# Masks of attention scores in row halves, value products ahead of transposes, and one root-mean-square pair per item

## The chip, the cores and the metric

The kernel runs on one core of one Trainium2 chip. The metric is the device time of one execution in microseconds (us), here the median of several runs. One more execution was recorded by the hardware profiler, and every row below is from it. The engines are TensorE (PE; its weight loads are listed apart as PEld), VectorE (DVE), ScalarE (ACT), GpSimd (POOL) and SyncE (SP).

## The reference

64 items of audio go through a convolution tower (four convolutions with channel norms), an importance pooling that leaves 128 rows of 64 numbers per item, causal attention, and a mixture of experts. Only the attention is touched by the change:

```python
x = layernorm(h)                                   # (64, 128, 64)
q = (x @ wq.T) as 16 heads of 64; k, v = x @ wkv.T # one key/value head for all 16
q = rmsnorm(rope(q), q_norm_w); k = rmsnorm(rope(k), k_norm_w)
scores = q @ k.T / 8                               # 128 x 128 per head
scores = where((cols <= rows) & (rows - cols <= 128), scores, -1e30)   # causal: T is 128
h = h + (softmax(scores) @ v over the heads) @ wo.T
```

So each of 64 items has 16 heads with a 128 x 128 score matrix, 1024 such matrices in all.

## The kernel before

The program has a convolution phase (0 to about 720 us) and a token phase, which interleaves three streams by an order written out by hand: importance and pooling, attention, experts. Each engine walks the same list of slots `u` and issues in each slot what is planned for it. Work goes from engine to engine by semaphores, and each engine does its instructions strictly in order.

In the attention a slot is one *part* (four heads of one item): 256 slots, from 1034 us to about 1740 us. Two slots make a *half* `m` (eight heads); scores are issued once a half, on even slots. Below, "pair" means these two slots, and pairs are numbered by `m % 8`, since everything repeats after 8 pairs (4 items, a *quad*). In steady state an item passes through these steps:

- **Queries.** `project(m)` (L1163, L1164) makes eight heads of queries in PSUM; DVE applies the rotation (`rope_q`, L1277 to L1279); ACT squares (`square`, L1417) and DVE sums the squares (`sum_q`, L1310); ACT makes the reciprocal root by a Ln and an Exp (`rms_q`, L1423 and L1428), once a half; POOL adds the two rotated products (`add_q`, L1545) and multiplies by the root (`scale_q`, L1552); PE transposes (`q_t`, L1173) and ACT copies out (`keep_q`, L1435). The slots are in the tables `at_q`, `at_rms`, `at_qm`, `at_qt`.
- **Scores.** `scores(m)` fills two PSUM banks. For each bank, one bf16 matmul of the identity with the mask (128 rows, 512 columns; L1186) writes the mask, and then the products with the keys are added (L1191). These use 64 rows of the array, the two banks' products in different row halves. Three banks rotate, so `scores(m)` waits for the exponentials of part `2m-2`.
- **Softmax.** DVE takes the negated maximum (`maximum`, L1317), ACT the exponentials with their sums (`exps`, L1446), DVE the reciprocal (`recip`, L1325), POOL multiplies (`normalize`, L1559).
- **Transposes and value products.** PE transposes each part three slots later (`p_t`, L1203) into the one bank TB, DVE copies it out (`p_copy`, L1332), and the next `p_t` waits for that copy. `p_v` (L1214) multiplies eight heads by the values, on even slots: two column halves of the array of 64 columns each. `w_o` (L1224) is the output projection of a quad, of the same column halves, in four pieces `c`, in slots 6, 7, 8 and 9 of every 16.
- **Once a quad** PE also does `x_t`, `k_v`, `k_t` and `turn` (L1131 to L1151, L1234), DVE `rope_k`, `sum_k`, `residual`, `statistics`, and POOL the preparation of the keys and of the next quad's input.

The order in a slot on PE is: `scores`, `p_t`, `project`, `q_t`, `x_t`, `k_v`, `k_t`, `w_o`, `turn`, `p_v`. On DVE: `maximum(u)`, `recip(u-1)`, `p_copy(u-3)`, `rope_q`, `sum_q`, then the quad's pieces. On ACT: `keep_o`, `square`, `keep_q`, `rms_q`, the quad's pieces, `exps(u)`. On POOL: `normalize(u-1)`, `add_q`, `scale_q`, the quad's pieces.

Of the kernel before, what the change touches and what calls it, by code (L numbers as in the profile page):

```python
# [8 lines left out]
BF16 = mybir.dt.bfloat16  # L9
F32R = mybir.dt.float32r  # L10
U32 = mybir.dt.uint32
ALU = mybir.AluOpType
# [4 lines left out]
B = 64  # L17
# [6 lines left out]
NH, DH = 16, 64  # L24
# [18 lines left out]
          ("riota", 8), ("eps0", 1), ("scaled", 1)]  # L43
# [26 lines left out]
def audio_tower(nc, A, out):  # L70
    const_at, n_const = offsets(CONSTS)
    with ExitStack() as ctx:
# [3 lines left out]
        def sem(name):  # L76
# [35 lines left out]
        identb = sb("identb", [128, 128], BF16)  # L112
        maskb = sb("maskb", [128, 4, 128], BF16)
# [14 lines left out]
                 cs=cs, mv=mv, rstd=rstd, wqkv=wqkv, wo=wo, wqk=wqk, identb=identb, maskb=maskb, fcol=fcol, fwr=fwr,  # L128
# [489 lines left out]
def importance_pool_phase(nc, V, sem, ctx):  # L618
# [252 lines left out]
    def vector(ve):  # L871
# [81 lines left out]
        def stats4(i):  # L953
# [7 lines left out]
            for r in range(4):  # L961
# [3 lines left out]
        ve.tensor_copy(V["identb"][:], K["ident"])  # L965
        ve.tensor_copy(V["maskb"][:], K["mask"].unsqueeze(1).to_broadcast([128, 4, 128]))
        ve.scalar_tensor_tensor(out=V["wqk"][:], in0=V["qkw"][:, 0:DH], scalar=float(DH) ** -0.5,
                                in1=V["qkw"][:, DH:2 * DH], op0=ALU.mult, op1=ALU.mult)
# [69 lines left out]
def attention_phase(nc, V, sem, ctx, kept, pool):  # L1038
# [4 lines left out]
    wqkv, wo, wqk, identb, maskb = V["wqkv"], V["wo"], V["wqk"], V["identb"], V["maskb"]  # L1043
# [25 lines left out]
    at_q = by_slot(HALVES, lambda m: 4 * (m // 2) - 11 + 2 * (m % 2))  # L1069
    at_rms = by_slot(HALVES, lambda m: 4 * (m // 2) - 9 + 2 * (m % 2))  # L1070
# [4 lines left out]
    at_wo = {16 * (q + 1) + 6 + c: (q, c) for q in range(QUADS) for c in range(4)}  # L1075
# [43 lines left out]
    def tensor(pe):  # L1119
# [57 lines left out]
        def scores(m):  # L1177
# [7 lines left out]
            for bank in banks:  # L1185
                pe.matmul(bank, identb[:], maskb[:].rearrange("p a s -> p (a s)"), start=True, stop=False,  # L1186
                          skip_group_check=True)
# [9 lines left out]
        def p_t(n):  # L1197
            i, k = n // 4, n % 4
            if n >= 1:
                pe.wait_ge(S["pT"], n)  # L1200
            pe.wait_ge(S["pn"], n + 1)
            for h in range(4):
                last = pe.transpose(ps[:, TB, h * T:(h + 1) * T], pb[:, i % 2, 4 * k + h, :], K["ident"])  # L1203
            last.then_inc(S["pt"], 1)

# [32 lines left out]
        def slot(u):  # L1238
# [9 lines left out]
            if u == min(at_pt):  # L1248
                pe.wait_ge(made["h4"], QUADS)
            if u == min(at_pv):  # L1250
                pe.wait_ge(made["wx"], QUADS)
            if u in at_pt:
                p_t(at_pt[u])
# [19 lines left out]
    def vector(ve):  # L1273
# [83 lines left out]
        def prepare():  # L1357
            high, low = split(ve, wh[:], wl[:], wqkv[:])
# [30 lines left out]
    def scalar(ac):  # L1389
# [74 lines left out]
        def slot(u):  # L1464
# [16 lines left out]
            if u - 1 in at_wo and at_wo[u - 1][1] == 3:  # L1481
                keep_y(at_wo[u - 1][0])
# [5 lines left out]
    def gpsimd(po):  # L1488
# [58 lines left out]
        def scale_q(m):  # L1547
            h = m % 2
            po.wait_ge(S["rq"], m + 1)
# [607 lines left out]
def shape_constants():  # L2157
# [8 lines left out]
            "ones": np.ones((128, 128)), "mask": np.where(j <= i, 0.0, -1e30),  # L2166
# [4 lines left out]
    return np.concatenate([np.asarray(cols[n], np.float32) for n, _ in CONSTS], 1)  # L2171
# [71 lines left out]
```

## Time and profile before

| | us |
|---|---|
| runs, median of 3 (1931.29 to 1932.2) | 1932.19 |
| profiled execution, its own time | 1930.25 |
| span of the profile (first to last instruction) | 1928.3 |
| PE busy / share | 1816.9 / 94% |
| DVE busy / share | 1525.3 / 79% |
| ACT busy / share | 1354.8 / 70% |
| POOL busy / share | 921.0 / 48% |

Busy times are unions of intervals over the whole span; the shares are averages over stages that differ. The mean granted clock of TensorE was 0.982 of its full speed.

### The profile page before, as it was taken

The page shows a single profiled execution, that of the slowest core. Times are in us where ns is not written, and L with a number is a line of the kernel's source. Part 1 is how long each engine was busy: PE and PEld are TensorE (multiplying, and loading weights), DVE is VectorE, ACT ScalarE, POOL GpSimd, SP SyncE. Part 2 cuts the span into 40 slices and gives each one's busy share as a digit, 9 for nine tenths or more (in the row PEclk, how much of TensorE's full clock was granted, in tenths as well). Part 3 has the DMA queues.
Part 4 walks back from the last instruction along what each step waited for, and adds up shares of the span by engine and source line. Part 5 has one row for each costly group of instructions (what it writes and reads, how often), then busy time and mean ns, then how long its engine had stood idle before and what let it go on. Part 6 is the DMA issues. An engine that isn't in the chain of part 4 may idle for free.

```text
span 1928.3 us, 35012 instructions
## 1 busy us (share of the span) xinstructions
PE 1816.9 (94%) x10533; PEld 1276.7 (66%) x10533; DVE 1525.3 (79%) x3372; ACT 1354.8 (70%) x3865; POOL 921.0 (48%) x1544
## 2 busy tenths in 40 slices
PE   3999999999999968999997999999999999999998
PEld 2777888888878856877875666666655555664443
DVE  5788888888888856566657888888999988896665
ACT  1567667767767653444436999999998999986765
POOL 1222322322322210022247989988888899983200
PEclk9999999999999988999987999999999999999999
DMA  3311111111111000000000000000000000004554
GB/s 97 96 45 38 34 47 37 35 49 34 37 47 34 25 1 1 0 1 1 1 1 1 2 2 2 2 2 2 1 2 2 2 2 2 2 2 181 188 214 166
DMA packets 30518, 69.02 MB, mean 36 GB/s; under 512 B 14108, under 2 KB 14748, under 8 KB 28028
## 3 DMA queue, kind: packets, MB, share of 16 engines
q1 hardware_dynamic: 30332, 66.78, 10.7%
q8 instruction: 87, 1.43, 0.3%
q14 instruction: 99, 0.81, 0.1%
HBM read 45.12 MB, written 2.36 MB: 25 GB/s over the span
## 4 chain that ended last, share of the span: by engine, by line
PE 37%; DVE 12%; issue 6%; POOL 4%; ACT 3%; DVEq 0%; POOLq 0%; ACTq 0%
PE ps L1191 4%; PE ps L65 4%; PE ps L1203 3%; PE ps L67 3%; PE ps L66 3%; PE ps L1224 3%; PE ps L1762 3%; PE ps L1214 2%; DVE amx L1317 2%; PE ps L1186 2%; DVE apT L1332 2%; PE ps L1173 2%; DVE assq L1310 1%; POOL apb L1559 1%; DVE atq L1277 1%
## 5 line engine op out<-in xcount | busy, mean ns | idle before, releaser
L1446 ACT ACTIVATE apb<-ps,amx 128x128 f32<-128x128 f32 x1024 | 360.0, 366 | 47.0 <-DVE amx L1317 46.5
L1559 POOL TENSOR_TENSOR apb<-apb,arc 128x512 f32<-128x512 f32 x256 | 268.4, 1048 | 43.9 <-DVE arc L1325 43.6
L1317 DVE TENSOR_REDUCE amx<-ps 128x4 f32<-128x512 f32 x256 | 174.4, 681 | 59.7 <-PE ps L1191 58.5
L1446 ACT ACTIVATION_READ_ACCUMULATOR apb<-ps,amx 128x1 f32 x1024 | 210.4, 205 | 0.0
L583 POOL TENSOR_TENSOR h0h<-h0h,const 128x1 fp32r<-128x1 f32 x256 | 46.6, 217 | 338.8 <-DVE h0l L479 338.8
L65 PE MATMUL ps<-h0h,w123h 128*128 128x512 f32 x512 | 203.0, 396 | 0.0
L67 PE MATMUL ps<-h0h,w123l 128*128 128x512 f32 x512 | 202.5, 396 | 0.0
L66 PE MATMUL ps<-h0l,w123h 128*128 128x512 f32 x512 | 202.5, 395 | 0.0
L1203 PEld LDWEIGHTS ps<-const,apb 128*128 128x128 f32 x1024 | 107.3, 140 | 135.9 <-DVE apT L1332 109.6
L479 DVE SCALAR_TENSOR_TENSOR h0l<-ps,h0h 128x1024 fp32r<-128x1024 f32 x128 | 156.0, 1219 | 46.3 <-ACT h0h L383 46.3
L1203 PE MATMUL ps<-const,apb 128*128 128x128 f32 x1024 | 167.6, 286 | 18.7 <-DVE apT L1332 18.0
L1332 DVE COPY apT<-ps 128x512 f32<-128x512 f32 x256 | 170.0, 664 | 6.8 <-PE ps L1203 6.5
L1191 PEld LDWEIGHTS ps<-akT,aqT 64*128 64x128 f32 x2048 | 125.0, 188 | 54.7 <-issue 54.7
L1191 PE MATMUL ps<-akT,aqT 64*128 64x128 f32 x2048 | 149.6, 286 | 0.0
L383 ACT ACTIVATE h0h<-ps 128x1024 fp32r<-128x1024 f32 x128 | 129.9, 1015 | 24.9 <-PE ps L307 24.9
L1214 PE MATMUL ps<-apT,avs 128*64 128x512 f32 x512 | 136.6, 612 | 0.0
L807 ACT ACTIVATE z<-ps,mcol 128x512 f32<-128x512 f32 x64 | 44.1, 689 | 114.8 <-PE ps L67 114.8
L1012 POOL TENSOR_TENSOR part<-cs,const 128x512 f32<-128x512 f32 x16 | 18.3, 1142 | 214.5 <-DVE cs L925 213.2
L67 PEld LDWEIGHTS ps<-h0h,w123l 128*128 128x128 f32 x512 | 97.0, 189 | 22.5
L66 PEld LDWEIGHTS ps<-h0l,w123h 128*128 128x128 f32 x512 | 97.4, 190 | 18.8
L1830 ACT ACTIVATE apb<-ps,mw 128x512 f32<-128x512 f32 x128 | 81.0, 687 | 40.8 <-PE ps L1749 40.5
L65 PEld LDWEIGHTS ps<-h0h,w123h 128*128 128x128 f32 x512 | 97.0, 189 | 18.8 <-DVE sq1b L498 0.4
(320 smaller groups left out, 5065.9 us busy)
## 6 DMA issues: line engine op xcount, KB each, us to landing
h<-gates SPq DMA_DIRECT2D x8, 2048.0 KB, 7.1
atq<-gates SPq DMA_DIRECT2D x8, 2048.0 KB, 7.3
x0k<-x0h SPq DMA_DIRECT2D x128, 72.0 KB
x<-in_x SPq DMA_DIRECT2D x32, 192.0 KB, 2.6
x0k<-x0l SPq DMA_DIRECT2D x64, 72.0 KB
x0k<-x0h SPq DMA_DIRECT2D x64, 48.0 KB
out<-akT SPq DMA_DIRECT2D x16, 128.0 KB, 1.9
x0k<-x0l SPq DMA_DIRECT2D x32, 48.0 KB
```

What stands on the lines that cost most here:

```text
L65: pe.matmul(out, wh, xh, start=start, stop=False)
L66: pe.matmul(out, wh, xl, start=False, stop=False)
L67: return pe.matmul(out, wl, xh, start=False, stop=stop)
L383: ac.activation(padded(h0h, row, half, i), ps[:, Y0:Y0 + 2, :], ACT.Relu).then_inc(s_h0h, 1)
L479: ve.scalar_tensor_tensor(out=padded(h0l, row, half, i), in0=ps[:, Y0:Y0 + 2, :], scalar=0.0, in1=padded(h0h, row, half, i).bitcast(F32), ...
L1191: last = pe.matmul(bank[:, p * T:(p + 1) * T], qT[rows, i % 2, 4 * h + p, :], kT[rows, i // 4 % 2, i % 4, :], start=False, stop=True, skip ...
L1203: last = pe.transpose(ps[:, TB, h * T:(h + 1) * T], pb[:, i % 2, 4 * k + h, :], K["ident"])
L1214: last = pe.matmul(ps[64 * odd:64 * odd + 64, OB, :], vs[:, i // 4 % 3, i % 4, :], pT[:, 8 * h + 4 * odd:8 * h + 4 * odd + 4, :], start=Tr ...
L1317: ve.tensor_reduce(mx[:, n % 4, :], ps[:, SB[n % 3], :].rearrange("p (h s) -> p h s", h=4), AX_X, ALU.max, negate=True).then_inc(S["mx"], 1)
L1332: ve.tensor_copy(pT[:, 4 * k:4 * k + 4, :], ps[:, TB, :].rearrange("p (h t) -> p h t", h=4)).then_inc(S["pT"], 1)
L1446: last = ac.activation(pb[:, i % 2, head, :], ps[:, SB[n % 3], h * T:(h + 1) * T], ACT.Exp, bias=mx[:, k, h:h + 1], accum_out=sm[:, i % 2, ...
L1559: po.tensor_tensor(p, p, rc[:, i % 2, 4 * k:4 * k + 4].unsqueeze(2).to_broadcast([T, 4, T]), ALU.mult).then_inc(S["pn"], 1)
```

## The change

- The mask of two banks is written by four matmuls in place of two. Each uses 64 rows and 256 columns (4 heads by 64 keys) of bf16; the bank of even heads uses the lower 64 rows, the other bank the upper ones, as the score products do. A new constant `maskt` (which row of the mask a query takes) and a folded `maskb` replace the identity and the full mask; they are made in `prepare`, in the middle of the importance phase, and `identb`, `maskb` and `wqk` are no longer made at the phase's start. Two constant columns are added.
- On PE the order in a slot becomes: `scores`, `p_v`, `w_o`, `p_t` on even slots, `project`, `q_t`, `x_t`, `k_v`, `k_t`, `turn`, `p_t` on odd slots. `w_o` has two pieces each in slots 6 and 8 in place of one in slots 6 to 9, and `keep_y` follows one slot earlier.
- `rms_q` does both halves of an item by one Ln and one Exp of 16 columns, in the slot of the first of the two before. `project`, `rope_q`, `square`, `sum_q` and `add_q` are two slots earlier.
- Waits that follow: `rms_q(i)`'s Exp waits for `scale_q` of both halves of the item before, and `sum_q` for the Ln of the item before.

```diff
-    at_q = by_slot(HALVES, lambda m: 4 * (m // 2) - 11 + 2 * (m % 2))
-    at_rms = by_slot(HALVES, lambda m: 4 * (m // 2) - 9 + 2 * (m % 2))
+    at_q = by_slot(HALVES, lambda m: 4 * (m // 2) - 13 + 2 * (m % 2))
+    at_rms = by_slot(B, lambda i: 4 * i - 9)
-    at_wo = {16 * (q + 1) + 6 + c: (q, c) for q in range(QUADS) for c in range(4)}
+    at_wo = {16 * (q + 1) + 6 + c: ((q, c), (q, c + 1)) for q in range(QUADS) for c in (0, 2)}
...
-            for bank in banks:
-                pe.matmul(bank, identb[:], maskb[:].rearrange("p a s -> p (a s)"), start=True, stop=False,
-                          skip_group_check=True)
+            for n in range(2):
+                for a, bank in enumerate(banks):
+                    rows = slice(a * DH, (a + 1) * DH)
+                    pe.matmul(bank.rearrange("p (h s) -> p h s", h=4)[:, :, n * DH:(n + 1) * DH], maskt[rows, n, :],
+                              maskb[rows, n, :, :], start=n == 0, stop=False, skip_group_check=True)
...
+            if u in at_pv:
+                p_v(at_pv[u])
+            for c in at_wo.get(u, ()):
+                w_o(*c)
+            if u % 2 == 0:
+                turn_p(u)
             if u in at_q:
                 project(at_q[u])
...
-            if u in at_wo:
-                w_o(*at_wo[u])
             if u in at_tr:
                 turn(at_tr[u])
-            if u in at_pv:
-                p_v(at_pv[u])
+            if u % 2 == 1:
+                turn_p(u)
...
-                ve.wait_ge(S["lrq"], m - 1)
+                ve.wait_ge(S["lrq"], i)
...
+            ve.tensor_copy(maskt[0:DH, 0, :], K["ident"][0:DH, :])
...
+            ve.tensor_copy(maskb[:], K["mask"].rearrange("p (n s) -> p n s", n=2).unsqueeze(2
+                                                                                         ).to_broadcast([T, 2, 4, DH]))
...
-        def rms_q(m):
-            i, h = m // 2, m % 2
-            heads = slice(8 * h, 8 * h + 8)
-            ac.wait_ge(S["ssq"], m + 1)
-            ac.activation(lrq[:, heads], ssq[:, heads], ACT.Ln, bias=epsc[:, 1:2], scale=1.0 / DH
-                          ).then_inc(S["lrq"], 1)
-            ac.wait_ge(S["lrq"], m + 1)
+        def rms_q(i):
+            ac.wait_ge(S["ssq"], 2 * i + 2)
+            ac.activation(lrq[:], ssq[:], ACT.Ln, bias=epsc[:, 1:2], scale=1.0 / DH).then_inc(S["lrq"], 1)
+            ac.wait_ge(S["lrq"], i + 1)
             if i >= 1:
-                ac.wait_ge(S["qm"], m - 1)
-            ac.activation(rq[:, heads], lrq[:, heads], ACT.Exp, scale=-0.5).then_inc(S["rq"], 1)
+                ac.wait_ge(S["qm"], 2 * i)
+            ac.activation(rq[:], lrq[:], ACT.Exp, scale=-0.5).then_inc(S["rq"], 1)
```

`turn_p(u)` is the old call of `p_t` with its wait, under a name.

## Rows read from the trace of the kernel before

**Rows 1.** Busy time of each engine in ten periods of attention: length, engines, clock, DMA.

```profile
1100.00:1540.00 440.00, 429.03 (x3226) 263.91 (x3224) 391.25 (x954) 400.30 (x1718) 393.08 (x399) 1.00 0.01 2
```

**Rows 2.** Waits in that stretch: who waited for whom, us, times, longest.

```profile
PEld ps L1203 <- DVE apT L1332: 69.4, 72, 1.9
```

**Rows 3.** PE's timeline over one period: start, us, instructions, [idle before].

```profile
1313.88 0.59 PE L1186 MATMUL ps<-maskb,identb 128*128 128x512 bf16 x2
...
1316.09 1.08 PE L1224 MATMUL ps<-h,wo 128*64 128x512 f32 x4
...
1319.44 1.08 PE L1224 MATMUL ps<-h,wo 128*64 128x512 f32 x4
...
1327.04 0.60 PE L1186 MATMUL ps<-maskb,identb 128*128 128x512 bf16 x2
1327.57 1.16 PE L1191 MATMUL ps<-akT,aqT 64*128 64x128 f32 x16
1328.66 0.66 PE L1203 MATMUL ps<-const,apb 128*128 128x128 f32 x4
1329.25 1.08 PE L1214 MATMUL ps<-apT,avs 128*64 128x512 f32 x4
1330.26 0.66 PE L1203 MATMUL ps<-const,apb 128*128 128x128 f32 x4
1330.67 0.47 PE L1163 MATMUL ps<-wh,axx 128*128 128x512 f32 x1
...
1331.65 0.60 PE L1234 MATMUL ps<-const,aysb 128*128 128x128 f32 x4
1332.09 0.59 PE L1186 MATMUL ps<-maskb,identb 128*128 128x512 bf16 x2
...
1337.16 0.59 PE L1186 MATMUL ps<-maskb,identb 128*128 128x512 bf16 x2
...
1342.01 0.59 PE L1186 MATMUL ps<-maskb,identb 128*128 128x512 bf16 x2
...
1347.91 0.61 PE L1186 MATMUL ps<-maskb,identb 128*128 128x512 bf16 x2
...
1352.54 0.59 PE L1186 MATMUL ps<-maskb,identb 128*128 128x512 bf16 x2
...
1356.47 0.66 PE L1203 MATMUL ps<-const,apb 128*128 128x128 f32 x4 [0.65 <-DVE apT L1332]
...
1357.87 0.59 PE L1186 MATMUL ps<-maskb,identb 128*128 128x512 bf16 x2
```

**Rows 4.** DVE's timeline over one pair: first and last instruction of ten.

```profile
1328.76 0.69 DVE L1317 TENSOR_REDUCE amx<-ps 128x4 f32<-128x512 f32 x1 [1.59 <-PE ps L1191]
...
1332.81 0.41 DVE L1279 TENSOR_TENSOR atq<-ps,const 128x256 f32<-128x256 f32 x1
```

**Rows 5.** ACT's timeline: the end of exponentials, and the Ln and Exp of the roots.

```profile
1319.49 0.21 ACT L1428 ACTIVATE arq<-alrq 128x8 f32<-128x8 f32 x1
...
1330.87 0.61 ACT L1455 ACTIVATE h<-ps 128x512 f32<-128x512 f32 x1
...
1331.35 0.32 ACT L1423 ACTIVATE alrq<-assq,epsc 128x8 f32<-128x8 f32 x1
1331.70 0.21 ACT L1428 ACTIVATE arq<-alrq 128x8 f32<-128x8 f32 x1
```

**Rows 6.** POOL's timeline: two multiplications of queries by their roots.

```profile
1318.96 1.05 POOL L1552 TENSOR_TENSOR aqr<-aqr,arq 128x512 f32<-128x512 f32 x1
...
1330.61 1.04 POOL L1552 TENSOR_TENSOR atq<-atq,arq 128x512 f32<-128x512 f32 x1
```

**Rows 7.** DVE's timeline at the start of the token phase.

```profile
723.61 0.23 DVE L965 CAST identb<-const 128x128 bf16<-128x128 f32 x1 [1.61 <-PEq L141]
...
724.22 0.42 DVE L59 CAST mw1h<-mw 128x512 fp32r<-128x512 f32 x1
```

**Rows 8.** PE's timeline at the same place.

```profile
730.00 0.79 PE L65 MATMUL ps<-mxh,mw1h 128*128 128x512 f32 x1 [9.48 <-DVE mw2l L60]
```

More of the change, by code:

```diff
@@ L42 @@
           ("stri", 128), ("ones", 128), ("mask", 128), ("iota", 64), ("ropec", 64), ("ropes", 64),
-          ("riota", 8), ("eps0", 1), ("scaled", 1)]
+          ("riota", 8), ("eps0", 1), ("scaled", 1), ("low", 1), ("lower", 1)]
 PARAMS = ["b1", "b2", "b3", "g0", "g1", "g2", "g3", "g4", "e0", "e1", "e2", "e3", "e4"]
@@ L111, in audio_tower @@
         epsc = sb("epsc", [128, 3])
-        identb = sb("identb", [128, 128], BF16)
-        maskb = sb("maskb", [128, 4, 128], BF16)
+        maskt = sb("maskt", [128, 2, 128], BF16)
+        maskb = sb("maskb", [128, 2, 4, 64], BF16)
         wqk = sb("wqk", [128, DH])
@@ L963, in stats4 @@
             last.then_inc(S["mv"], 1)
[L965 to L968, printed above, removed]
         for n, (h, l, w) in enumerate(((w1h, w1l, mw1), (w2h, w2l, mw2))):
@@ L1042, in attention_phase @@
     h4, mv, rstd = V["h4"], V["mv"], V["rstd"]
-    wqkv, wo, wqk, identb, maskb = V["wqkv"], V["wo"], V["wqk"], V["identb"], V["maskb"]
+    wqkv, wo, wqk, maskt, maskb = V["wqkv"], V["wo"], V["wqk"], V["maskt"], V["maskb"]
     T, QK, HH = C, NH * DH, NH // 2
@@ L1204, in p_t, with turn_p @@
             last.then_inc(S["pt"], 1)
+        def turn_p(u):
+            if u == min(at_pt):
+                pe.wait_ge(made["h4"], QUADS)
+            if u in at_pt:
+                p_t(at_pt[u])
         def p_v(m):
@@ L1357, in prepare @@
         def prepare():
+            ve.tensor_copy(maskt[0:DH, 0, :], K["ident"][0:DH, :])
+            ve.tensor_copy(maskt[DH:T, 0, 0:DH], K["ident"][DH:T, DH:T])
+            ve.tensor_copy(maskt[DH:T, 0, DH:T], K["ident"][DH:T, 0:DH])
+            ve.tensor_scalar(maskt[0:DH, 1, DH:T], K["ident"][0:DH, 0:DH], K["low"][0:DH, :], None, ALU.mult)
+            ve.tensor_scalar(maskt[DH:T, 1, DH:T], K["ident"][DH:T, DH:T], K["low"][DH:T, :], None, ALU.mult)
+            ve.tensor_scalar(maskt[:, 1, 0:DH], K["ones"][:, 0:DH], K["lower"], None, ALU.mult)
+            ve.tensor_copy(maskb[:], K["mask"].rearrange("p (n s) -> p n s", n=2).unsqueeze(2
+                                                                                         ).to_broadcast([T, 2, 4, DH]))
+            ve.scalar_tensor_tensor(out=wqk[:], in0=V["qkw"][:, 0:DH], scalar=float(DH) ** -0.5,
+                                    in1=V["qkw"][:, DH:2 * DH], op0=ALU.mult, op1=ALU.mult)
             high, low = split(ve, wh[:], wl[:], wqkv[:])
@@ L1480, in slot @@
                 keep_k(at_kt[u - 1])
-            if u - 1 in at_wo and at_wo[u - 1][1] == 3:
-                keep_y(at_wo[u - 1][0])
+            for q, c in at_wo.get(u - 1, ()):
+                if c == 3:
+                    keep_y(q)
             if 0 <= u < PARTS:
@@ L1548, in scale_q @@
             h = m % 2
-            po.wait_ge(S["rq"], m + 1)
+            po.wait_ge(S["rq"], m // 2 + 1)
             po.wait_ge(S["qr"], m + 1)
@@ L2165, in shape_constants @@
             "gmask": same / (C - 1.0), "blkones": same, "tri": i <= j, "stri": i < j,
-            "ones": np.ones((128, 128)), "mask": np.where(j <= i, 0.0, -1e30),
+            "ones": np.ones((128, 128)), "mask": np.where((j % 64 <= i % 64) & ((j < 64) | (i % 64 < 63)), 0.0, -1e30),
+            "low": i % 64 < 63, "lower": i % 64 == 63,
             "iota": np.broadcast_to(np.arange(TN), (128, TN)),
@@ L2170, in shape_constants @@
             "riota": np.broadcast_to(E - np.arange(E), (128, E))}
-    return np.concatenate([np.asarray(cols[n], np.float32) for n, _ in CONSTS], 1)
+    return np.concatenate([np.asarray(cols[n][:, 0:w], np.float32) for n, w in CONSTS], 1)
 def patch_index():
```

6 lines of the change are left out of this document (1 added, 5 removed).

## The prediction

> **What bounds the kernel now.** I read three views in this order. First the busy times by stretch: in a steady part of the attention PE is busy 429.0 of 440.0 us, ACT 400.3, POOL 393.1, DVE 391.3, at full clock and with the DMA engines at 1% [rows 1]. Second the list of waits: the largest by far is PE's weight load of the transposes (L1203) on DVE's copy of the bank before them, 69.4 us in 72 waits [rows 2]; but it is a wait of the loads, and most of it lies under matmuls that still run. Third PE's timeline. It repeats every 8 pairs: the mask (L1186) starts at 1313.88 and, eight pairs on, at 1357.87, so a period is 43.99 us, and 16 of them are the attention's 704 us [rows 3]. The first two pairs, which hold the output projection, take 13.16 us together; the next six take 5.05, 5.07, 4.85, 5.90, 4.63 and 5.33. In the last one stands the largest idle, 0.65 us before a transpose; another of 0.17 is in the pair of 4.85. So PE works 43.99 - 0.82 = 43.17 us a period. PE bounds the attention, with a small loss to DVE's copy. Per period the others are busy 39.1 (DVE), 40.0 (ACT) and 39.3 (POOL), a tenth of what 440 us hold [rows 1]. This is the number to keep in mind: PE can gain some 3 to 4 us a period before it is no longer alone.
>
> **Masks in row halves.** From a mask's start to the scores is 0.53 us, at 1327.04 to 1327.57 [rows 3]. The new form has the same 1024 columns in four matmuls, in pairs on different rows and banks. Do such pairs overlap? The 16 score products have 128 columns each and take 1.09 us, 68 ns each; the four transposes L1234, of 128 columns on the full array, take 0.44, 110 ns each. So two do run at once. What a mask costs is then half of what its columns cost: 0.53 less about 0.10 for the change of array shape behind it (next paragraph) is 0.43, and half of it 0.21 is saved. Bounds: 0, if the four run one after another (the same 1024 columns), and 0.27, half of the whole row. I take 0.21, since the scores right behind use just these row halves.
>
> **Changes of shape.** The transposes between scores and value products take 0.59 us (1328.66 to 1329.25), the same four of one size without a change of shape 0.44 (1331.65 to 1332.09) [rows 3]. A change thus costs 0.15. In the order before a plain pair has four: full array to rows (mask to scores), to full (transposes), to columns (value products), to full. Afterwards it has three: full to rows (ahead of the mask), rows to columns, columns to full. A pair with the output projection has six before (L1224 at 1316.09 touches the value products, L1224 at 1319.44 stands alone) and three afterwards. Saved: 0.15 in each of six pairs and 0.45 in each of two. Bounds: 0, if going from rows to columns costs twice, and 0.15 per change as taken. The Trainium skill, "TensorEngine Tiling (Array Packing)", Key Properties, says that a change of the tiling mode, not of the tile alone, drains the TensorE. By that rule it is the count of changes that pays, and the sum would be the one just made; the trace agrees with 0.15 us a change.
>
> **PE's sum.** Six pairs by 0.21 + 0.15 and two by 0.21 + 0.45 are 2.16 + 1.32 = 3.48 us a period: 43.17 becomes 39.7. The plain pair of 4.63 becomes 4.27, and two pairs with the projection 13.16 - 1.32 = 11.84.
>
> **One root per item.** A Ln takes 0.35 up to the Exp behind it and the Exp about 0.12 more before the next exponential starts (1331.35, 1331.70) [rows 5]; four pairs of them less a period are 1.8 to 1.9 us on ACT, 40.0 to 38.2. ACT idles before the exponentials now, so this alone is worth nothing; it keeps ACT from being the next bound. In the time it is 0.
>
> **Moves.** `project`, the rotation, squares, sums and `add_q` start two slots earlier with the same instructions and no DMA; no queue of SP is passed. They are paced by the same slots, so their cost is 0; at the start of the attention one more of them stands before the first scores and its first starts two slots sooner, plus or minus 1 us. The two projection pieces moved to an even slot stand ahead of the even transposes and delay them by 2 us twice a period; what waits for those is DVE's copy, which has had the maximum and the sums to do meanwhile.
>
> **Start of the phase.** Three DVE instructions go from 723.61 to 724.22 [rows 7], ahead of the splits that PE waits for with 9.48 us idle [rows 8]: 0.6 us saved, on the path. What replaces them, six small ones and a copy of 512 columns, is about 1.4 us by the two durations of [rows 7], in the middle of the importance phase behind a larger split of weights. DVE has gaps there, so it is hidden; uncovered it is 1.4, once.
>
> **Where the stall goes.** The order of PE before gives the odd transposes 1.0 us after the even ones (the value products, 1329.25 to 1330.26), while DVE has first a maximum and a reciprocal to do after the scores and only then the copy. That is why lateness of DVE shows as idle PE at once. Afterwards the value products come first, the copy's input is there when DVE has done the maximum, and the odd transposes follow projection and query transposes (1330.67 to 1331.65, 0.98 us). DVE may then be about 1 us late there. The next tight place is the scores: they wait for the exponentials of the part before, which ended at 1330.87, 2.2 us after the scores' end at 1328.66 [rows 3, 5]; PE's new work between is 1.01 + 0.44 + 0.98 + 0.59 = 3.0. So lateness of up to 0.5 to 0.8 us is carried. DVE's plain pair is from 1328.76 to the end of 1332.81's, 4.38 to 4.46 us [rows 4]: more than PE's new 4.27. Its quad work comes on top, 39.1 - 8 x 4.38 = 4.1 us, of which I estimate 3.3 in the five pairs that have no large PE extra (rotation and sum of the keys, residual and statistics), the rest in the others. In these five PE needs 24.92 - 0.82 - 5 x 0.36 = 22.3 (5.05 + 5.07 + 4.85 + 4.63 + 5.33 less its idle), DVE 21.9 + 3.3 = 25.2. The gap of 2.9 can be carried into the following heavier pairs twice, by 0.5 each: 1.9 us of PE idle. The same reckoning for the order before, with 0.3 carried, is 25.2 - 24.1 - 0.6 = 0.5, where the trace shows 0.82. I take 2.0 for the new one.
>
> **The sum.** 39.7 + 2.0 = 41.7 against 43.99: 2.3 us a period. Of the 16 periods I count 15, since the last ten pairs have DVE's gates of the experts among them and the first are start-up: 34.5 us, and 0.6 from the phase's start, makes 35. Against the profiled execution (span 1928.3, own time 1930.25) that is a span of 1893 and a time of 1895; the median of the runs is 1.9 higher than that execution, so 1932.2 - 35 = **1897 us**. A difference of 0.2% (3.9 us) is about what a measurement of this kernel can tell from none.
>
> **The rivals.**
>
> *A: the other engines follow better, or the idle goes.* PE at 39.7 and idle no more than the 0.8 of before: 3.4 us by 15.5 periods and 0.6 is 53: 1879. For it: POOL at 39.3 and DVE at 39.1 would just fit. Against it: DVE's plain pair alone is longer than PE's. 17% for a time under 1884.
>
> *B: the others take more.* DVE, POOL and ACT can't carry 0.5 us, or the row halves of the mask don't overlap. Without overlap PE is at 41.4, DVE's stalls shrink to about 0.9, the period is 42.3 and the time 1932 - 0.6 - 15 x 1.7 = 1906. With nothing carried each pair takes its slowest engine: 11.84, DVE's 25.2 and PE's 5.90 - 0.36 = 5.54 make 42.6, and 1932 - 0.6 - 15 x 1.4 = 1910; ACT's quad work in the same pairs adds to it, some 0.5 a period, 1918. The Trainium skill, "TensorEngine Tiling (Array Packing)", PSUM Bottleneck, speaks against this change in this sense: tiling speeds up TensorE but not the evacuation of PSUM, whose copies may become the bottleneck. By that the DVE row of 4.38 to 4.46 would set the pair. 18% for 1910 to 1928.
>
> *C, slower: ACT's Exp waits for POOL.* The Exp of an item's roots now needs `scale_q` of the slot right before, no longer one three slots back, and behind it on ACT stand the exponentials of that part, and so the reciprocal, `normalize` and in the end the transposes. At 1331.70 the Exp starts 0.05 after that multiplication ends (1330.61 + 1.04); at 1319.49 it starts 0.52 before its end (1318.96 + 1.05) [rows 5, 6]. With the times of now that is some 0.5 us a wait in part of 64 items, hidden in ACT's idle. But POOL is at 39.3 of 41.7: if it is late by a whole multiplication more, the wait is 1.0 to 1.5 us and sits on the path. 35 us over 64 items are 0.55 each: from there it decides. At 1.1 us each on the path the time is 1897 + 70 - 30 (the 2.0 us a period of DVE's stall, which it covers) = 1937. 5%.
>
> *D: no change to be told,* if gain and waits cancel. 3%.
>
> **Chances and range.** The forecast, 1884 to 1910, 57%; A 17%, B 18%, C 5%, D 3%. Faster is the forecast with A and B, 92%; same 3%, slower 5%. The range reaches from A's 1879 to B's 1918: 1879 to 1918.
>
> **What would show it.** In the trace of the changed kernel: a period of about 41.7 us between every eighth mask; four mask matmuls of 256 columns in about 0.2 to 0.3 us (right) or 0.45 (wrong); plain pairs of 4.4; the two projection pairs at 5.9 each; PE idle of 2 us a period before transposes on DVE's copy, or before scores on the exponentials; ACT's busy time less by 1.8 a period. It is wrong if the mask row keeps its length, if L1428 shows waits on POOL with PE idle behind them, or if the six light pairs keep their lengths of before.

## The result, and the profile after

The changed kernel takes 1941.0 us (median of 5 runs, 1939.97 to 1943.22), the kernel before 1932.2 (5 runs): a ratio of 1.0046, interval 1.0033 to 1.0059. It is slower by some 9 us, where 35 us less was forecast; at less than half a per cent that is a small loss, but the interval stays above 1. The profiled execution has a span of 1938.4 us against 1928.3.

I read the same views again. First the busy times of the same stretch of attention:

```profile
1100.00:1540.00 440.00, 412.28 (x3408) 264.42 (x3404) 398.06 (x964) 389.05 (x1658) 396.89 (x402) 1.00 0.01 2
```

PE's busy time fell from 429.0 to 412.3 us, while DVE and POOL rose from 391.3 and 393.1 to 398.1 and 396.9 [rows 1]: the same stretch holds only a little more work. PE is no longer full, and on the average of this stretch nothing else is. (A mean hides stages: in the light pairs behind the output projection DVE has no listed wait, from 1332.67 to 1353.62 in its timeline.) Then the largest waits, in the same stretch:

```profile
DVE apT L1336 <- PE ps L1201: 28.0, 29, 1.9
PEld ps L1159 <- ACT atq L1431: 26.5, 51, 1.2
...
ACT atq L1431 <- DVE atq L1283: 22.3, 58, 0.4
PEld ps L1184 <- ACT apb L1457: 21.9, 63, 0.9
```

Before, PE waited for DVE's copy [rows 2]. Now DVE's copy waits for PE's transposes (L1201), PE's projection waits for ACT's square (L1431), the square waits for DVE's rotation (L1283), and PE's mask (L1184) waits for ACT's exponentials. PE's timeline over one period shows what came of it:

```profile
1322.07 0.39 PE L1184 MATMUL ps<-maskb,maskt 64*128 64x256 bf16 x4 [0.28 <-ACT apb L1457]
1328.04 0.39 PE L1184 MATMUL ps<-maskb,maskt 64*128 64x256 bf16 x4
1334.01 0.39 PE L1184 MATMUL ps<-maskb,maskt 64*128 64x256 bf16 x4
1337.16 0.50 PE L1159 MATMUL ps<-wh,axx 128*128 128x512 f32 x1 [0.27 <-ACT atq L1431]
1339.13 0.39 PE L1184 MATMUL ps<-maskb,maskt 64*128 64x256 bf16 x4
1339.36 1.06 PE L1189 MATMUL ps<-akT,aqT 64*128 64x128 f32 x16
1340.35 1.08 PE L1218 MATMUL ps<-apT,avs 128*64 128x512 f32 x4
...
1344.17 0.39 PE L1184 MATMUL ps<-maskb,maskt 64*128 64x256 bf16 x4
1348.57 0.66 PE L1201 MATMUL ps<-const,apb 128*128 128x128 f32 x4 [0.37 <-DVE apT L1336]
1349.45 0.39 PE L1184 MATMUL ps<-maskb,maskt 64*128 64x256 bf16 x4 [0.22 <-ACT apb L1457]
1355.39 0.39 PE L1184 MATMUL ps<-maskb,maskt 64*128 64x256 bf16 x4
1360.02 0.39 PE L1184 MATMUL ps<-maskb,maskt 64*128 64x256 bf16 x4 [0.28 <-ACT apb L1457]
1363.86 0.50 PE L1159 MATMUL ps<-wh,axx 128*128 128x512 f32 x1 [0.96 <-ACT atq L1431]
1365.75 0.39 PE L1184 MATMUL ps<-maskb,maskt 64*128 64x256 bf16 x4 [0.28 <-ACT apb L1457]
```

The reader should see four things against [rows 3]. The four mask matmuls take 0.23 us (1339.13 to 1339.36) in place of 0.53. The two pairs with the output projection take 5.97 each in place of 13.16 together. The six light pairs take 5.12, 5.04, 5.28, 5.94, 4.63 and 5.73, where they took 5.05, 5.07, 4.85, 5.90, 4.63 and 5.33: one is shorter by 0.03, four are longer by 0.04 to 0.43, though PE has less to do in them. And the period is 1365.75 - 1322.07 = 43.68 us where it was 43.99.

So the steady part gained 0.3 us a period and not 2.3. Where are the other 10 us? The first mask starts at 1042.3 in place of 1034.1, 8 us late. The end of the convolution phase moves from execution to execution (by up to 3.5 us over all the traces here), so it is safer to count from the token phase's first matmul, in PE's timeline:

```profile
729.64 0.79 PE L65 MATMUL ps<-mxh,mw1h 128*128 128x512 f32 x1 [8.89 <-DVE mw2l L60]
```

From there to the first mask it is 312.6 us (729.64 to 1042.26), and 304.1 before (730.00 [rows 8] to 1034.06): 8.6 us more. The cause stands in POOL's timeline just before:

```profile
1011.88 1.28 POOL L1557 TENSOR_TENSOR atq<-atq 128x512 f32<-128x512 f32 x1 [22.84 <-DVE atq L1283]
1013.11 0.73 POOL L1529 TENSOR_TENSOR akr<-aka,akb 128x256 f32<-128x256 f32 x1
1013.80 1.04 POOL L1008 TENSOR_TENSOR part<-cs,const 128x512 f32<-128x512 f32 x1
```

`part` (L1008) is the first step of a weight job of the importance pooling, and the pooling's last steps lead up to the attention. POOL's timeline of the kernel before has the first of the last three jobs at 1005.65:

```profile
1005.65 1.04 POOL L1012 TENSOR_TENSOR part<-cs,const 128x512 f32<-128x512 f32 x1
```

Now `add_q` of the first half (L1557), two slots earlier, stands ahead of it in POOL's queue and waits for DVE's rotation. And at the end of the attention, where POOL also prepares the experts' input, ACT's Exp of the roots waits for POOL:

```profile
1696.85 0.22 ACT L1439 ACTIVATE arq<-alrq 128x16 f32<-128x16 f32 x1 [2.81 <-POOL atq L1564]
```

### The profile page after: what moved, and what is told of

Its sections match the earlier page's. It is cut to its first block, busy times and chain, and to the rows that moved or that the text cites. A ratio compares the mean times of both kernels' runs of the same rounds, so it can differ in the third digit from the quotient of the medians.

```text
span 1938.4 us, 35338 instructions
## 1 busy us (share of the span) xinstructions
PE 1786.7 (92%) x10789; PEld 1277.9 (66%) x10789; DVE 1530.3 (79%) x3377; ACT 1330.6 (69%) x3737; POOL 921.5 (48%) x1544
## 4 chain that ended last, share of the span: by engine, by line
PE 33%; DVE 10%; issue 7%; POOL 7%; ACT 5%; DVEq 0%; ACTq 0%; POOLq 0%
PE ps L65 4%; PE ps L67 3%; PE ps L66 3%; PE ps L1218 3%; PE ps L1774 3%; PE ps L1201 3%; PE ps L1189 2%; ACT apb L1457 2%; PE ps L1228 2%; POOL apb L1571 2%; DVE atq L1281 1%; PE ps L1760 1%; DVE assq L1314 1%; DVE apT L1336 1%; PE ps L1184 1%
## 5 line engine op out<-in xcount | busy, mean ns | idle before, releaser
L1457 ACT ACTIVATE apb<-ps,amx 128x128 f32<-128x128 f32 x1024 | 365.3, 384 | 24.2 <-DVE amx L1321 23.5
L1457 ACT ACTIVATION_READ_ACCUMULATOR apb<-ps,amx 128x1 f32 x1024 | 228.9, 224 | 0.0
L1336 DVE COPY apT<-ps 128x512 f32<-128x512 f32 x256 | 172.8, 675 | 51.4 <-PE ps L1201 48.9
L1201 PEld LDWEIGHTS ps<-const,apb 128*128 128x128 f32 x1024 | 110.5, 141 | 120.5 <-issue 90.9
L1201 PE MATMUL ps<-const,apb 128*128 128x128 f32 x1024 | 164.2, 283 | 8.7 <-DVE apT L1336 8.6
L1189 PE MATMUL ps<-akT,aqT 64*128 64x128 f32 x2048 | 137.6, 275 | 0.0
L1008 POOL TENSOR_TENSOR part<-cs,const 128x512 f32<-128x512 f32 x16 | 18.3, 1143 | 214.0 <-DVE cs L925 212.7
```

The source lines that it names most:

```text
L1189: last = pe.matmul(bank[:, p * T:(p + 1) * T], qT[rows, i % 2, 4 * h + p, :], kT[rows, i // 4 % 2, i % 4, :], start=False, stop=True, skip ...
L1336: ve.tensor_copy(pT[:, 4 * k:4 * k + 4, :], ps[:, TB, :].rearrange("p (h t) -> p h t", h=4)).then_inc(S["pT"], 1)
L1457: last = ac.activation(pb[:, i % 2, head, :], ps[:, SB[n % 3], h * T:(h + 1) * T], ACT.Exp, bias=mx[:, k, h:h + 1], accum_out=sm[:, i % 2, ...
```

## The experiments

All times of the twelve experiments are medians. "The period" is eight pairs from mask to mask (from scores to scores where records of masks are missing), each pair taken as the median over its places in the steady part; for the kernel before it is 43.97, for the changed kernel 43.63 us. "The last 15 pairs" are the scores of halves 112 to 127: 83.1 before, 87.0 changed. "The start" is the time from the token phase's first matmul to the first mask (304.1 before, 312.6 changed), and "the attention" that from the first mask to the last (703.0 before, 705.0 changed); both are read from one trace of each version. The kernel before ran beside each group of experiments: 1932.7 us beside the first four, 1931.3 beside the next four, 1930.3 beside the last four. So times of different groups compare to about 2 us.

### One repair at the start: `add_q` behind the weights

```diff
+    at_add = {}
+    for u, m in at_q.items():
+        at_add.setdefault(max(u, -10), []).append(m)
...
-            if u in at_q:
-                add_q(at_q[u])
+            for m in at_add.get(u, ()):
+                add_q(m)
```

> The changed kernel, with POOL's add_q of the first item (both halves) issued in slot -10, behind the last weights of the importance pooling, and nothing else. Theory: in the changed kernel add_q of half 0 stands in slot -13, one slot ahead of the last three weight jobs, so POOL waits for the rotation (done at about 1011.6) and these jobs start at 1013.6 in place of 1005.7, and the end of the pooling and the first scores come 7.8 us late. Then the first scores start at about 1034.5 in place of 1042.5 and the time is 1941 - 8 = 1933. Rival: it is the seventh project, rotation and square ahead of the first scores, a chain of 3.3 us each on PE, DVE and ACT, that delays the start; then nothing moves and the time stays at 1940 to 1942.

Measured: 1936.5 us (1930.8 to 1939.6, 10 runs), ratio to before 1.0017, interval 1.0007 to 1.0027. POOL's timeline shows the first of the three weight jobs no longer behind the rotation:

```profile
1001.97 1.04 POOL L1008 TENSOR_TENSOR part<-cs,const 128x512 f32<-128x512 f32 x1
...
1014.76 2.50 POOL L1560 TENSOR_TENSOR atq<-atq 128x512 f32<-128x512 f32 x2
```

and the phase's first matmul and the first mask, in PE's timeline, are

```profile
728.00 0.79 PE L65 MATMUL ps<-mxh,mw1h 128*128 128x512 f32 x1 [8.89 <-DVE mw2l L60]
...
1034.13 0.39 PE L1187 MATMUL ps<-maskb,maskt 64*128 64x256 bf16 x4
```

The place of the first scores is the 1034.1 of the kernel before, but the token phase began 2.0 us sooner in this execution. The start is 306.1 us: 6.5 less than in the changed kernel and still 2.1 more than before. So the theory holds for three quarters of the delay. The remaining 2 us are no accident of this trace: the starts of the five versions with this repair are 306.1 to 306.8 us, those of the six versions with the queries in their old slots 303.6 to 304.5. The rival, one more projection, rotation and square ahead of the first scores, may be their cause; no run separates it. The median fell by 4.5 us and the profiled span by 9.0, to 1929.4 (6.5 of it at the start, 1.6 by a convolution phase that ended sooner, 1.3 in the attention, less 0.4 at the end). The steady period stayed at 43.62.

### The masks alone

The kernel before with the mask loop of the change, `maskt`, and their making in `prepare`; nothing else.

> The kernel before with the masks in row halves alone (with maskt and the folded mask made in prepare); order of PE, root pairs and query slots as before. In the changed kernel's trace a mask with the scores and the change of shape ahead takes 1.78 us where it took 2.06, so PE sheds 0.28 us a pair, 2.2 a period of 43.99. Theory: PE is the bound in the order before and DVE can follow with about 1 us of idle on PE: period 41.8 to 42.2, time 1900 to 1906. Rival: the other engines are the bound as soon as PE is faster, whatever the order: period 43.0 or more, time 1916 or more.

Measured: 1909.4 us (4 runs), ratio 0.9883 (0.9869 to 0.9898). The period is 42.24, between the theory's 41.8 to 42.2 and the rival's 43.0, at the theory's end; the time is 3 us above the theory's 1906 and clear of the rival's 1916. The plain pair of 4.63 fell to 4.30 and the heavy ones, with the output projection, from 6.58 to 6.18. The busy times and the waits of the same stretch:

```profile
1100.00:1540.00 440.00, 419.50 (x3510) 271.01 (x3506) 404.32 (x984) 413.73 (x1780) 408.21 (x414) 1.00 0.01 2
```

```profile
PE ps L1201 <- DVE apT L1330: 19.9, 37, 2.0
```

PE's wait for DVE's copy grew from 10.9 us in the kernel before to 19.9. DVE, ACT and POOL rose to 404 to 414 of 440: they can follow PE beyond the changed kernel's pace. One part of the change, alone, makes the kernel 23 us faster; the attention is 680.2 us, 22.8 less than before.

### PE's order alone

The kernel before with the order `scores`, `p_v`, `w_o` (two pieces), even `p_t`, the rest, odd `p_t`; full masks, roots as before.

> The kernel before with PE's new order alone (value products and doubled output projection ahead of the even transposes, odd transposes last in the slot); full masks, root pairs and query slots as before. Theory: the order saves PE 0.15 us in each of six pairs and 0.45 in two, 1.8 a period, but DVE, strictly in order, stands before its copy until the even transposes are done, 1 us later in plain pairs and 2.8 later in the two with the projection, and with it the next maximum, the rotation, ACT's square and exponentials; so the gain is lost: period 43.5 to 44.5, time 1925 to 1940. Rival: the order is harmless and what ate the gain is the wait of the Exp on POOL: period 42.2 to 42.6, time 1903 to 1910.

Measured: 1942.5 us (4 runs), ratio 1.0053 (1.0038 to 1.0068). The period is 44.74, above even the theory's upper end of 44.5, and the time above its 1940. The two heavy pairs fell from 6.58 to 6.28 each, so the saved changes of shape are there; all the light ones but one grew or stayed, the third from 5.33 to 6.03. The rival falls. The attention is 714.5 us, 11.6 more than before. The largest wait of DVE for another engine is

```profile
DVE apT L1338 <- PE ps L1203: 42.7, 40, 2.4
```

### The roots and the queries' slots alone

The kernel before with one Ln and one Exp of 16 columns per item, and `project` and what follows it two slots earlier, as in the change; nothing else.

> The kernel before with one root pair per item and the queries' chain two slots earlier alone; full masks and PE's order as before. Theory: it costs the 8 us at the start (POOL's add_q ahead of the last weights) and nothing in the steady part: period 43.9 to 44.1, time 1938 to 1942. Rival: the Exp's wait for scale_q of the slot before stops ACT for up to 0.5 us in each item and delays the exponentials: period 44.5 to 45.5, time 1948 to 1965.

Measured: 1943.3 us (4 runs), ratio 1.0055 (1.004 to 1.007). The period is 43.97, as before, and the last 15 pairs take 84.4; the start is 312.9 us (with the first mask at 1044.4, since the phase itself began 1.5 us later here than in the trace of before); the attention is 703.2, 0.2 more than before. So nearly all of its harm is the start. The waits of ACT's Exp on POOL, 0.7 us at the longest in this stretch, are there but hidden, with PE in its old order and full masks:

```profile
ACT arq L1425 <- POOL aqr L1549: 9.8, 18, 0.7
```

### Masks and order without the roots

> Masks in row halves and PE's new order, with the roots and the queries' slots as before. The order alone lengthened the period to 44.74 and the masks alone shortened it to 42.24. Theory: the order's harm is DVE's blocked copy and does not need the late roots, so this has the changed kernel's period, 43.4 to 43.8, with the start of before (first scores at 1034.5) and no loss in the last items: time 1926 to 1930. Rival: the Exp's wait on POOL is what costs the steady part with the new order, then the period is 42.5 or less and the time under 1912.

Measured: 1920.9 us (4 runs), ratio 0.9946 (0.9931 to 0.9961), period 43.30, last 15 pairs 85.1. Better than the theory's 1926 by 5 us and far from the rival's 1912. The attention is 693.6 us: the order costs 13.4 against masks alone (1.06 a period; 11 in the medians). Against the first experiment (period 43.62, attention 703.7) the roots cost 10.1 us once PE is in its new order; in the medians of the pairs they show as 0.32 a period, all of it in the pair with `k_v`, 5.88 against 5.57.

### DVE's queue fitted to PE's order

```diff
-            if u in at_pt:
-                p_copy(at_pt[u])
             if u in at_q:
                 rope_q(at_q[u])
             if u - 1 in at_q:
                 sum_q(at_q[u - 1])
+            if u in at_pt:
+                p_copy(at_pt[u])
```

> The changed kernel with add_q of the first item in slot -10 (as in the first experiment), and DVE's queue in another order: on even slots the sum of squares and on odd slots the rotation stand ahead of the copy of the transposes. No instruction is added or taken away. Theory: DVE stands idle before the even copy (1.45 us in pairs with the output projection, about 0.6 in others) because its queue is strictly in order; with 0.6 us of other work put there, and the rotation no longer behind the odd copy, the rotation, square, exponentials and masks come earlier: period 43.6 to 41.5 or 42.5, time 1905 to 1920. Rival: DVE, ACT or POOL are simply full, whatever the order; then the period stays within 0.3 of 43.6 and the time is 1931 or more.

Measured: 1911.8 us (4 runs), ratio 0.9898 (0.9881 to 0.9914), against 1936.5 without this edit: 25 us for putting one call behind two others (23 by the ratios). The period fell from 43.62 to 42.10, the attention from 703.7 to 682.6. In the changed kernel DVE's timeline in a pair with the output projection is

```profile
1324.48 0.68 DVE L1321 TENSOR_REDUCE amx<-ps 128x4 f32<-128x512 f32 x1
1325.08 0.17 DVE L1329 RECIPROCAL arc<-asm 128x4 f32<-128x4 f32 x1
1326.70 0.69 DVE L1336 COPY apT<-ps 128x512 f32<-128x512 f32 x1 [1.45 <-PE ps L1201]
1327.31 0.68 DVE L1314 TENSOR_REDUCE assq<-atq 128x8 f32<-128x512 f32 x1
```

The sum of squares (L1314) has its input and stands behind a copy (L1336) that has not, for 1.45 us. With the edit the sum stands ahead, but in a pair with the output projection the copy still waits:

```profile
1357.70 0.68 DVE L1324 TENSOR_REDUCE amx<-ps 128x4 f32<-128x512 f32 x1
1358.29 0.17 DVE L1332 RECIPROCAL arc<-asm 128x4 f32<-128x4 f32 x1
1358.38 0.67 DVE L1317 TENSOR_REDUCE assq<-atq 128x8 f32<-128x512 f32 x1
1360.54 0.69 DVE L1339 COPY apT<-ps 128x512 f32<-128x512 f32 x1 [1.49 <-PE ps L1204]
```

The 0.6 us that I expected before the copy in the other pairs is not there: the changed kernel has 0.18, once a period. So little idle was filled, and the theory's account is too narrow. The waits from 1100 to 1540 us tell what changed. Without the edit (first experiment):

```profile
DVE apT L1339 <- PE ps L1204: 28.0, 29, 1.9
...
ACT atq L1434 <- DVE atq L1286: 21.8, 57, 0.4
...
PE ps L1162 <- ACT atq L1434: 13.1, 21, 1.0
```

With it:

```profile
DVE apT L1339 <- PE ps L1204: 24.5, 18, 1.5
...
PE ps L1204 <- DVE apT L1339: 20.6, 34, 0.9
```

DVE's wait for the transposes fell by 3.5 us in ten periods. PE's projection no longer waits for ACT's square, nor the square for DVE's rotation; PE waits for the copy again, as with the masks alone. The gain of 1.5 us a period goes with the loop of rotation, square and projection. The edit puts two things ahead of the copy, the sum on even slots and the rotation on odd ones; no run separates them, and these waits speak for the rotation.

### A second buffer for the roots

```diff
-    rq = sb("arq", [T, NH])
+    rq = sb("arq", [T, 2, NH])
...
-            if i >= 1:
-                ac.wait_ge(S["qm"], 2 * i)
-            ac.activation(rq[:], lrq[:], ACT.Exp, scale=-0.5).then_inc(S["rq"], 1)
+            if i >= 2:
+                ac.wait_ge(S["qm"], 2 * (i - 1))
+            ac.activation(rq[:, i % 2, :], lrq[:], ACT.Exp, scale=-0.5).then_inc(S["rq"], 1)
```

> The changed kernel with add_q of the first item in slot -10 and a second buffer for the roots, so that the Exp waits for scale_q of two items before, not of the item before. Theory: the wait costs where POOL also has the experts' input to prepare: the last 15 pairs go from 86.7 to about 83.5 us; in the steady part PE's idle comes from DVE's blocked copy, so the period stays 43.4 to 43.7. Time 3 to 5 us under the first experiment's. Rival: ACT's waits on POOL (12 us in 440) are on the path all along: the period falls to 42.5 and the time to 1915 or less.

Measured: 1923.8 us (5 runs), ratio 0.9965 (0.9952 to 0.9978). That is 12.7 us under the first experiment, where I expected 3 to 5, and 7.6 us in the profiled spans. The period fell by 0.32 to 43.30, just what the roots had cost, and the last 15 pairs from 86.7 to 84.8. In the traces the attention fell by 9.5 us, from 703.7 to 694.2: 0.6 in the first eight pairs, 7.0 in the next 104, 1.9 in the last 15. That is more than 13 periods of 0.32, since the medians leave out pairs that are longer only now and then. The spans differ by less, because the first experiment's token phase began 1.6 us sooner and its start was 0.7 shorter. So the wait costs some 7 us in the steady part too, less than the rival said and more than I did, and with the second buffer the attention is within 0.6 us of the version without the roots (693.6).

### Masks with the doubled projection in the old order

PE's order `scores`, `p_t`, ..., `w_o` (two pieces on even slots), `turn`, `p_v`.

> Masks in row halves with the old order of PE, but the output projection's pieces doubled on even slots, right ahead of the value products and behind the even transposes. Two changes of shape are saved in each of two pairs, 0.3 us each. Theory: DVE gets its even copy as early as before, so the gain shows: the two pairs go from 6.18 and 6.16 to about 5.9, the period from 42.24 to 41.6 or 41.8, the time to 1899 to 1904. Rival: the odd transposes, 2 us later in these pairs, hold DVE's odd copy and the rotation behind it, and the light pairs after them grow: period 42.2 or more, 1909 or more.

Measured: 1907.5 us (4 runs, 1904.1 to 1909.4), ratio 0.9876 (0.9861 to 0.9891), period 42.13. The two heavy pairs fell by 0.14 each, from 6.17 to 6.03, and one light pair grew by 0.17. Neither side was right. I probably counted one saved change of shape too many: the odd piece stood right before the mask, which is in row halves here, so that leaving it out saves one change and not two. 0.14 is about the 0.15 of one change; that is argued from the order, not shown. The gain over masks alone, 1.9 us, is not clear of the scatter.

### Three repairs together

> The changed kernel with all three repairs: add_q of the first item in slot -10, the second buffer for the roots, and DVE's sum and rotation ahead of the copies. Theory: the three costs are apart and add up: from the version with the first and third (period 42.10, last 15 pairs 85.9) the second buffer takes 0.3 a period and 1.5 to 2 at the end: period 41.7 to 41.9, time 1903 to 1908. Rival: POOL, at 41.2 of 44 us busy, is now the bound and the second buffer changes nothing: 1910 to 1913.

Measured: 1902.7 us (4 runs), ratio 0.9858 (0.9843 to 0.9872). The time is as expected, the way there is not: the period stays at 42.08, and the gain lies in the last 15 pairs, 85.9 to 82.5, and in the first eight, 44.2 to 41.5 us.

### Masks, order and DVE's queue, roots as before

> Masks in row halves, PE's new order and DVE's sum and rotation ahead of the copies, with the roots and the queries' slots as before. Theory: with DVE's queue fitted to it, PE's new order is no longer harmful: against the version with masks and new order (period 43.30, 1920.9 us) the period falls to 41.7 to 42.2 and the time to 1903 to 1908, no slower than masks alone (1909.4). Rival: the repair works only with the queries two slots ahead; in the old slots the sum of squares waits for ACT's square and DVE stands idle there in place of the copy: period 42.8 or more, 1915 or more.

Measured: 1904.8 us (4 runs), ratio 0.9865 (0.985 to 0.988), period 42.30 against the theory's 41.7 to 42.2; the time is inside the theory's 1903 to 1908. The rival falls: with its queue fitted, DVE serves the new order without the roots' slots too.

### Masks, doubled projection and the repaired roots in the old order

> Masks in row halves, PE's old order with the doubled output projection, one root pair per item with the queries two slots ahead, add_q of the first item in slot -10, and the second buffer for the roots. Theory: PE waits here for DVE's copy only (21 us in 440), so ACT's 1.8 us less a period bring nothing: period 42.0 to 42.2, time 1904 to 1909. Rival: ACT's share counts now that PE is faster: period 41.6 or less, 1900 or less.

Measured: 1904.6 us (4 runs), ratio 0.987 (0.9854 to 0.9887), period 41.92, a tenth below what the theory gave; the time is inside. Against the version without the roots (1907.5) the medians differ by 2.9 us, which is not clear of the scatter. In the traces the attention is 7.1 us shorter (678.6 to 671.5) and the start 2.2 longer. So the roots do bring something once they have their second buffer; the theory's "nothing" was too low and the rival's period of 41.6 was not reached.

### DVE's new queue under PE's old order

> Masks in row halves with PE's old order, and DVE's sum and rotation ahead of the copies. Theory: what counts is which engine's next work stands behind what in a strict order. In the old order the odd transposes wait for the even copy, 1.0 us after the even ones; with 0.6 us of sums ahead of that copy PE waits more: period from 42.24 to 43.2 or more, time 1922 or more. Rival: DVE is simply better off with this queue in any order of PE (earlier rotation, earlier squares): period 42.0 or less, time 1907 or less.

Measured: 1956.6 us (4 runs, 1954.0 to 1963.2), ratio 1.0139 (1.012 to 1.0159), period 45.64. The same edit that gave 25 us under the new order costs 47 under the old one, against masks alone. The waits turned round with it:

```profile
PE ps L1201 <- DVE apT L1330: 49.5, 75, 2.4
...
DVE atq L1275 <- PE ps L1160: 36.7, 54, 2.4
```

PE waits 49.5 us for the copy that now stands behind other work, and DVE 36.7 us for the projection that PE issues behind those transposes.

## Why the prediction was wrong

**Where the 45 us went.** The forecast was 35 us less; the spans differ by 10 the other way. The traces of the parts divide it. *Masks:* forecast 1.68 us a period, 25 in 15 periods; measured 22.8 in the attention. *Order:* forecast 1.8 a period saved and some 1.2 of idle added, 9 us gained; measured 13.4 lost, on top of the masks. *Roots:* forecast 0; measured 11.4 lost in the attention (705.0 against 693.6). *Start:* forecast 0, plus or minus 1; measured 8.6 lost. These shares hold for parts added in this sequence: on the kernel before, the order alone cost 11.6 in the attention and the roots alone 0.2.

**The mask's term was right in kind and too small, the term for the changes of shape too large.** Forecast 0.21 us a pair by overlap of the row halves; the masks alone took 0.33 off the plain pair of 4.63 and 0.40 off the heavy ones. The mask row fell from 0.53 to 0.23, and the change of shape moved from behind it to ahead of it. The matmuls do overlap. For the order 0.45 was forecast in a heavy pair; behind the masks it took off 0.21 (6.18 to 5.97). The heavy pairs were forecast at 5.92 and took 5.97, but that agreement is two errors that cancel. The plain pairs' 4.27 was never reached: with the new order the shortest took 4.34, in the version with DVE's queue fitted.

**The step that failed first: "Where the stall goes".** It said that the order gives DVE room, since the odd transposes come later. It had in it, one sentence apart, the two facts that refute it: the value products stand ahead of the even transposes, and "lateness of up to 0.5 to 0.8 us is carried" by the scores. With `p_v` and `w_o` first, the input of DVE's even copy comes 0.9 us later in plain pairs and 2.6 us later in heavy ones (from the scores' start to the transposes' it is 2.00 and 3.72 us, where it was 1.09), and DVE, strictly in order, stands before it with its maximum done. In the changed kernel's trace it does so in the heavy pairs, for 1.45 and 1.49 us in every period, and hardly in the others (0.18 once a period). "Moves" said of this copy that DVE "has had the maximum and the sums to do meanwhile"; the sums stand behind the copy in DVE's queue. So the lateness that DVE was to carry from the light pairs into the heavy ones, twice 0.5 us, can't be worked off there: DVE idles. I took the copy's readiness as the thing that matters and asked how late DVE *may* be, not what the order *makes* it. The order alone costs 0.77 a period (44.74 against 43.97), though PE's own work falls. Putting DVE's copy behind two other calls brings back 1.5 us a period, and the same move under the old order costs 3.4 (45.64 against 42.24): this pair of runs shows that it is the order of the queues against each other, and neither DVE's load nor PE's order by itself. By which loop it acts is shown less well: DVE's wait for the transposes stays at 24.5 us of 28.0, and what goes away is the wait of PE's projection for rotation and square.

**The carried idle was mis-sized with it.** I forecast 2.0 us of PE idle; the period of 43.63 less PE's 39.7 by the sum is 3.9. The trace lists 2.8 a period as idle (440 less 412.3, over ten); the rest stands in starts that come later than they could without being listed, such as 0.80 us from the transposes to the projection (1341.36 to 1342.16) against 0.41 in a heavy pair (1326.01 to 1326.42). The reckoning "in these five PE needs 22.3, DVE 25.2" was tested only against an order in which DVE's copy was never blocked.

**The step that failed second: "Moves".** It priced the earlier queries at 0, plus or minus 1 us. It was 8.6 us at the first scores, and it was there to be read: POOL runs the importance weights and the attention from one queue, and slot -13 lies one slot ahead of the last three weight jobs. I checked that no DMA queue was passed and did not list what is queued behind `add_q` on POOL. The first experiment puts just these two instructions behind the weights and takes 6.5 us back. Some 2 us stay in all five versions that have this repair and the queries two slots earlier, and their cause is open.

**The step that failed third: "One root per item", priced at 0, and rival C with it.** Rival C had the right mechanism. ACT's Exp does wait for `scale_q` of the slot before; at the end of the attention for 2.81 us once. With PE's new order the second buffer takes 9.5 us out of the attention, 7.0 of them in the 104 pairs of the steady part and 1.9 in the last 15; with the old order and full masks the roots cost 0.2 there. I gave it 70 us if it decided, and 5%; its time of 1937 is near the measured 1941 by luck, since most of the loss came from the order and the start.

**Rival B had a part of it.** Its "with nothing carried" gave a period of 42.6: 11.84 for the heavy pairs, DVE's 25.2 for five light ones, 5.54 for the pair with `k_v`. The trace shows 11.94, 25.8 (5.12, 5.04, 5.28, 4.63 and 5.73) and 5.94; of the last 0.32 is the roots' wait. So nothing was carried, for the reason above. Whether DVE's own work sets the five light pairs is not shown: from 1332.67 to 1353.62 DVE has no listed wait, but with its queue fitted the same five take 24.6. DVE, ACT and POOL carry 404 to 414 us of work in 440 in the version with masks alone, and 389 to 398 in the changed kernel, so their mean load is not the bound. The Trainium skill's sentence on evacuation as the next bottleneck after a speedup of 4 times ("TensorEngine Tiling (Array Packing)", PSUM Bottleneck) fits that PE waits longer for DVE's copy once the masks are short (19.9 us, 10.9 before); the copies take 0.66 to 0.69 us in both kernels, and their duration was not what cost the time here.

**The sum as it came out,** by the profiled spans: the token phase began 0.4 us sooner; the start took 8.6 longer; the first eight pairs 1.1 longer, the next 104 were 3.0 faster, the last 15 3.9 slower, 2.0 together; the rest 0.1 shorter: 10.1 us, 1938.4 - 1928.3. PE's idle ahead of the phase's first matmul fell from 9.48 to 8.89 us, the 0.6 that was forecast for the phase's own start.

**What stays open.** The runs of the first experiment scatter over 9 us and its profile is at their low end, so the worth of its repair in the median is not better known than 4 to 9 us (6.5 at the start, in the traces). The scatter goes with the mean granted clock of TensorE: the two runs at 0.982 and 0.984 took 1930.8 and 1931.4 us, the eight at 0.976 to 0.980 took 1934.2 to 1939.6. What sets the clock of a run is not known. Three versions lie at 1902.7 to 1904.8 us with overlapping intervals, 1.3 to 1.4% below the kernel before; which of them is best can't be told.

## What to carry to other kernels

When instructions are moved ahead of others on one engine, write down for each consumer what stands behind it in its own strict queue, and move that queue along; the same reordering of DVE's queue was worth 25 us in one pairing and cost 47 in the other. A saving on the bound engine is worth what the loops through the other engines leave of it: test the parts of a change one by one, since here one part alone gave 23 us and the three together lost 9. A mean load over the whole stretch shows neither. An instruction that starts earlier in steady state starts earlier in the prologue too: look at what it overtakes there on every queue, above all on one shared with the stage before.

## What the runs showed of the hardware

Four bf16 matmuls of 64 rows and 256 columns, in pairs on the two row halves and two PSUM banks, took 0.23 us where two of 128 rows and 512 columns took 0.53 with the change of shape behind them. Going straight from row halves to column halves cost no more than going to the full array: scores to value products is 0.99 us in the changed kernel (1339.36 to 1340.35), and scores to transposes 0.99 us in the version with masks alone (1321.75 to 1322.74). In the kernel before, that distance is 1.09 [rows 3], with the change from the full array to row halves in it. PE showed 412 us busy of 440 in a stretch whose PE instructions take 1.5 us a period less once DVE's queue is fitted (42.10 against 43.62), so a share of 94% says little by itself.
